# Layer norms with logarithm and exponential on ScalarE in place of a square root, a reciprocal and a spread, in a six-layer transformer stack

## The reference

```python
x = x + 0.5 * L0_ffn(layernorm(x))      # A: coupled feed-forward
x = x + L0_attn(layernorm(x))           # B: causal attention, and a layer norm of its own (M)
x = x + 0.5 * L0_ffn(layernorm(x))      # C
x = x + 0.5 * L1_ffn(layernorm(x))      # D: 8 experts, top 2, and a shared one
x = x + L1_attn(layernorm(x))           # E: full attention
x = x + 0.5 * L1_ffn(layernorm(x))      # F
def layernorm(x): return (x - mean(x)) / sqrt(var(x) + 1e-5)
```

## Time and profile before

| | |
|---|---|
| median of 3 runs | 1381.76 us (1378.12 to 1389.53) |
| the profiled execution's own time | 1379.58 us |
| its span, first to last instruction | 1377.9 us |
| granted TensorE clock, mean | 0.974 |
| busy: TensorE, VectorE, ScalarE, POOL | 96%, 84%, 77%, 12% of the span |
| loop of the first attention | about 94 to 469 us |
| loop of the second attention | about 653 to 1286 us |

### The profile page before, as it was taken

The page is one execution under the profiler, slowest core; times in us unless marked ns, Lnnn a source line. Parts: engine busy times, 40 slices in busy tenths (PEclk is TensorE's granted clock), DMA queues, the critical chain, the costliest instruction groups (busy, mean ns, idle before and its releaser), DMA issues.

```text
span 1377.9 us, 30123 instructions
## 1 busy us (share of the span) xinstructions
PE 1317.6 (96%) x11896; PEld 470.0 (34%) x11896; DVE 1164.0 (84%) x1537; ACT 1054.4 (77%) x2060; POOL 165.7 (12%) x441
## 2 busy tenths in 40 slices
PE   8889999999999997999899999999999999999989
PEld 4243333332333352535233333332333323333533
DVE  6768889999999267555899999999999999995454
ACT  4548888998999636334499999999999999998431
POOL 9225221111111000001100000000000000000000
PEclk9989999999999999999699999999999999999899
DMA  5242310200000012001311000000000000000000
GB/s 144 54 132 43 46 21 21 42 5 12 4 4 5 12 31 62 1 0 47 115 48 49 4 4 12 4 4 3 12 4 4 4 4 11 4 4 3 11 7 24
DMA packets 38524, 35.09 MB, mean 25 GB/s; under 512 B 16080, under 2 KB 31920, under 8 KB 38384
## 3 DMA queue, kind: packets, MB, share of 16 engines
q1 hardware_dynamic: 38384, 33.17, 10.0%
HBM read 17.03 MB, written 9.70 MB: 19 GB/s over the span
## 4 chain that ended last, share of the span: by engine, by line
PE 53%; DVE 41%; ACT 2%; issue 2%; SPq 1%; DMA 0%; POOL 0%; DVEq 0%; ACTq 0%
DVE m_blockmax L1418 36%; PE ps L1296 10%; PE ps L1241 9%; PE ps L1277 7%; PE ps L1300 6%; PE ps L614 3%; PE ps L625 3%; PE ps L615 2%; PE ps L248 2%; PE ps L241 1%; PE ps L331 1%; PE ps L1260 1%; PE ps L235 1%; DVE m_xn L510 1%; DVE m_prob L506 1%
## 5 line engine op out<-in xcount | busy, mean ns | idle before, releaser
L1418 DVE TENSOR_REDUCE m_blockmax<-ps 128x2 f32<-128x1024 f32 (+1 forms) x768 | 880.9, 1207 | 24.4 <-PE ps L1241 18.3
L1391 ACT ACTIVATE m_prob<-ps 128x512 f32<-128x512 f32 (+3 forms) x1664 | 845.8, 576 | 48.5 <-PE ps L1277 34.2
L1277 PE MATMUL ps<-m_q_max,m_k_all 64*128 64x512 bf16 (+3 forms) x1664 | 338.2, 368 | 0.5
L1241 PE MATMUL ps<-m_k_all,m_q_all 64*128 64x512 bf16 (+3 forms) x1664 | 319.2, 382 | 19.4 <-DVE m_blockmax L1418 16.1
L1300 PE MATMUL ps<-m_prob,m_v_op 128*16 128x256 f32 x4096 | 320.9, 385 | 0.1
L1241 PEld LDWEIGHTS ps<-m_k_all,m_q_all 64*128 64x128 bf16 x1664 | 79.7, 93 | 344.7 <-DVE m_blockmax L1418 173.1
L1296 PE MATMUL ps<-m_prob,m_v_op 128*16 128x256 f32 (+3 forms) x2560 | 179.6, 353 | 0.8 <-POOL m_prob L1461 0.3
L1277 PEld LDWEIGHTS ps<-m_q_max,m_k_all 64*128 64x128 bf16 x1664 | 143.0, 94 | 90.8 <-ACT m_prob L1391 47.7
L1300 PEld LDWEIGHTS ps<-m_prob,m_v_op 128*16 128x16 f32 x4096 | 67.1, 94 | 133.7 <-issue 101.3
L1442 POOL CAST m_maxparts<-m_negmax 128x8 bf16<-128x8 f32 x64 | 14.1, 220 | 725.8 <-DVE m_negmax L1426 721.2
L724 ACT ACTIVATE m_prob<-ps 128x512 f32<-128x512 f32 x40 | 23.5, 594 | 71.4 <-PE ps L614 71.3
(11 more groups left out here) (221 smaller groups left out, 1033.2 us busy)
## 6 DMA issues: line engine op xcount, KB each, us to landing
m_part<-m_xn SPq DMA_DIRECT2D x48, 128.0 KB, 2.3
ba_parts<-m_part SPq DMA_DIRECT2D x8, 384.0 KB, 3.4
ea_parts<-m_part SPq DMA_DIRECT2D x8, 384.0 KB, 2.6
m_k_all<-ea_parts SPq DMA_DIRECT2D x84, 32.0 KB
m_q_all<-ea_parts SPq DMA_DIRECT2D x84, 32.0 KB
m_k_all<-ba_parts SPq DMA_DIRECT2D x36, 64.0 KB
m_q_all<-ba_parts SPq DMA_DIRECT2D x36, 64.0 KB
ba_sums<-m_pv SPq DMA_DIRECT2D x128, 9.0 KB
```

The source lines that it names most:

```text
L1241: mm = pe.matmul(ps[:, MX + 2 * (u % 2) + j, 0:width], q_all[head, pair, q0:q0 + TW], k_all[head, pair, CW * kc:CW * kc + width], start=Tr ...
L1277: pe.matmul(ps[:, e % ST, q0:CW], k_all[head, pair, TW * i:TW * i + TW], q_max[m % 2][head, q0:CW], start=True, stop=True).then_inc(self.s ...
L1391: nc.scalar.activation(prob[:, (2 * t + j) % NP, q0:CW], ps[:, e % ST, q0:CW], ACT.Exp, scale=SCALE)\
L1418: nc.vector.tensor_reduce(blockmax[:, m % plan.AHEAD, qt, :, kc], ps[:, MX + 2 * (u % 2):MX + 2 * (u % 2) + 2, 0:width], AX.X, ALU.max)\
```

## The change

1. The variance of a chunk comes from one product of all 512 columns with the same matrix of 1/128 as the mean, so it stands in all rows. `var_of`, `row_of`, `std`, `pe_spread` and `dve_invert` of the norm are gone. ScalarE takes Ln of the variance plus eps from PSUM into `sq`, then Exp with scale -0.5 in place. The norm's multiplication reads `sq`.
2. The warming calls ask for Ln where they asked for Sqrt. Square and root of successive chunks alternate in a different order. In `b_end` there are seven phases, and the first layer of the feed-forward for chunks 0 and 1 stands in the last (`ffn_c.pe(pe, True)`).
3. In attention B the builds of the first three pairs come before or right after the last queries and keys, in other banks (0, 1, 4, 5), the values' products are taken out of the opening and put behind the second to fifth `fill`, SP loads the first group after the parts of chunk 0, and middle copies of chunks 2 and 3 stand last on ScalarE.

```diff
     def pe_var(self, pe, i, c, bank):
         pe.wait_ge(self.squared, NC * i + c + 1)
-        for u in range(TPC):
-            mm = pe.matmul(self.ps[0:32, bank, 0:TW], self.k["var_of"][:, u, :], tile(self.k["sq"], TPC * c + u),
-                           start=(u == 0), stop=(u == TPC - 1))
-        mm.then_inc(self.var_ready, 1)
-
-    def pe_spread(self, pe, i, c, bank):
...
+        pe.matmul(self.ps[:, bank, :], self.k["mean_of"][:, :], chunk(self.k["sq"], c), start=True, stop=True)\
+            .then_inc(self.var_ready, 1)
...
-    def dve_invert(self, dve, i, c):
-        dve.wait_ge(self.std_ready, NC * i + c + 1)
-        self.nc.vector.reciprocal(self.std[:, c, :], self.std[:, c, :]).then_inc(self.inverted, 1)
...
+    def dve_norm(self, dve, i, c, dst):
+        dve.wait_ge(self.inverted, NC * i + c + 1)
+        self.nc.vector.tensor_tensor(chunk(dst, c), chunk(self.k["cen"], c), chunk(self.k["sq"], c), ALU.mult)\
             .then_inc(self.out, 1)
...
     def act_root(self, act, i, c, bank):
         act.wait_ge(self.var_ready, NC * i + c + 1)
-        self.nc.scalar.activation(self.std[:, c, :], self.ps[0:32, bank, 0:TW], ACT.Sqrt, bias=self.k["eps"][0:32, 0:1])\
-            .then_inc(self.std_ready, 1)
+        sq = chunk(self.k["sq"], c)
+        self.nc.scalar.activation(sq, self.ps[:, bank, :], ACT.Ln, bias=self.k["eps"][:, 0:1]).then_inc(self.logged, 1)
+        act.wait_ge(self.logged, NC * i + c + 1)
+        self.nc.scalar.activation(sq, sq, ACT.Exp, scale=-0.5).then_inc(self.inverted, 1)
...
+    def with_values(self, order):
+        out, fills = [], 0
+        for o in order:
+            out.append(o)
+            if o[0] == "fill":
+                fills += 1
+                if 2 <= fills < 2 + NC:
+                    out.append(("values", fills - 2, 0))
+        return out
...
         if self.causal and b == 0:
             pe.wait_ge(self.k["constants"].made, Constants.SELECT_MADE)
-            pe.wait_ge(self.rest_ready, 2 * NC)
-            pe.wait_ge(self.v_ready, NC)
+            pe.wait_ge(self.rest_ready, 2)
...
                 pe.wait_ge(self.k_built, pair + 1)
-                pe.wait_ge(self.q_built, pair + 1)
+                pe.wait_ge(self.q_built, 3)
...
@@ TensorE's program, ahead of attention B @@
                 att_b.pe_queries_keys(pe, 2)
-                att_b.pe_values(pe, 1)
+                att_b.pe_build(pe, 0)
+                att_b.pe_build(pe, 1)
                 pe.wait_ge(norm.out, NC * LN_B + 4)
                 att_b.pe_queries_keys(pe, 3)
-                att_b.pe_values(pe, 2)
-                att_b.pe_values(pe, 3)
-                for b in range(6):
+                for b in range(2, 6):
                     att_b.pe_build(pe, b)
...
@@ ScalarE's program, ffn_end and ahead of attention B @@
-                    warm(ACT.Sqrt)
-                    for c in range(3):
-                        norm.act_square(act, ln, c)
+                    warm(ACT.Ln)
+                    norm.act_square(act, ln, 0)
+                    norm.act_square(act, ln, 1)
                     norm.act_root(act, ln, 0, bank)
+                    norm.act_square(act, ln, 2)
+                    norm.act_root(act, ln, 1, bank + 1)
                     norm.act_square(act, ln, 3)
-                    for c in range(1, NC):
-                        norm.act_root(act, ln, c, bank + c)
+                    norm.act_root(act, ln, 2, bank + 2)
+                    norm.act_root(act, ln, 3, bank + 3)
                     warm(then)
...
-                att_b.act_values(act, 0)
-                for c in (2, 3):
-                    att_b.act_high(act, c)
-                    att_b.act_middle(act, c)
-                    att_b.act_values(act, c - 1)
-                att_b.act_values(act, 3)
-                for b in range(1, 6, 2):
-                    att_b.act_build(act, b)
+                att_b.act_high(act, 2)
+                att_b.act_build(act, 1)
+                att_b.act_high(act, 3)
+                att_b.act_build(act, 3)
+                att_b.act_build(act, 5)
+                att_b.act_middle(act, 2)
+                att_b.act_middle(act, 3)
                 att_b.act_loop(act)
```

More of the change, by code:

```diff
@@ L364, in pe @@
                 w1(s, 1)
-            if s == self.start and not begun:
-                for c in (2, 3):
-                    self.norm.pe_spread(pe, self.ln, c, c)
             if s > self.start:
@@ L666, in pe @@
                 down(i - 1)
-            if i == 1 and before is not None:
-                norm.pe_spread(pe, self.ln, NC - 1, self.BC)
             if i + 2 < len(steps):
@@ L825, in dve @@
         best(0, 1)
-        if before is not None:
-            self.norm.dve_invert(dve, self.ln, last)
-        else:
+        if before is None:
             logits(1)
@@ L831, in dve @@
         if before is not None:
-            self.norm.dve_norm(dve, self.ln, last, self.xn, self.BC)
+            self.norm.dve_norm(dve, self.ln, last, self.xn)
         shared(2)
@@ L1632, in _ @@
                     norm.pe_var(pe, LN_A, c, c)
-                pe.wait_ge(constants.made, Constants.ROWS_MADE)
-                for c in (0, 1):
-                    norm.pe_spread(pe, LN_A, c, c)
                 ffn_a.pe(pe, False)
```

192 lines of the change are left out of this document (72 added, 120 removed).

## The result

| | before | changed |
|---|---|---|
| median | 1383.83 us (1378.12 to 1389.53, 4 runs) | 1436.42 us (1430.97 to 1441.45, 4 runs) |
| ratio, 95% interval | | 1.0386 (1.0357 to 1.0416) |
| profiled execution, own time and span | 1379.58, 1377.9 us | 1437.54, 1435.8 us |
| granted TensorE clock, mean | 0.974 | 0.947 |

The change makes the kernel 3.9% slower, some 53 us by the medians and 58 us between the two profiled executions. The forecast was 1425 us, its range 1397 to 1446.

A forecast was written before the change was run, and what follows sets the result against it. The ending chain was TensorE 53%, VectorE 41%, ScalarE 2%. With two table loads per chunk, stage terms of 38.5 us plus 6 for clock took 1379.6 to 1424.1; with half of a 2.2 us offset, 1425; range 1397 to 1446.

The forecast's parts named there:

- The rival of one table: All chunk norms: Ln and Exp share one table, no load between them; sum -10.6 us, 1371 us; chance 0.13.
- first norm and ffn A: First layer norm into the feed-forward: ScalarE's four Ln-Exp pairs delay the first Gelu to 27.8 us; +7.3 us.
- norm before, and loop B: First attention: first score +0.2 us, then four value products moved into the loop cost 4.3; +4.5 us.
- after the first attention: Eight chunk norms in diagonal order: ScalarE's loads and waits for VectorE delay the first Gelu; +19.5 us, the largest term.
- norm before the first experts: The experts' Exp moves 4.0 us later, followed down to +0.9 at the sixth gate; +1.5 us.
- norms before the second attention: Chunks 2 and 3 are two whole pairs ahead of the second high copy, 651.4 instead of 646.74; +4.7 us.
- last experts: Norms before the last experts: norm 1 comes 0.9 us later, and the router with it; +1.0 us.
- clock, apart: All stages: TensorE's added idle time lowers its clock, doubling the cost of some products; +6 us, between 0 and 20.
- the step that took the transfer and the Tanh as the last things ahead of VectorE's update: First feed-forward: VectorE's update, held before by a transfer until 28.90, now waits for the Tanh and starts at 36.2.
- covered by the three windows built on the spot: First attention: SyncE's loads go out some 5 us later, but the fourth window, first to read them, comes near 108.
- The rival of the cold TensorE: Two loads, half clock across the first three norm stages and into feed-forwards: +20 for +6, 1439; chance 0.12 with builds.
- The builds don't come early: First attention: builds wait for the third build of queries, losing 7 us, 1432; chance 0.12 together with cold TensorE.

The follow-up runs named there:

- the joint set: Changed kernel, with the table set holding both Ln and Exp loaded by name before the norms, two warming calls removed: 1375.03 us, ratio 0.9933.
- The two queue runs: Changed kernel with SyncE's group 1 loads behind the first two sendings of sums: 1451.84 us; changed kernel with four sums buffers instead of two: 1435.53 us.
- the kernel with the joint set in this place alone: Changed kernel with the Ln-and-Exp set loaded by name only ahead of the eight chunk norms after the first attention: 1415.94 us, ratio 1.0230.
- the fillers: Changed kernel plus TensorE products whose results nobody reads: 96 of them, 1425.70 us, ratio 1.0306; 34 around the last experts only, 1434.18 us.
- the kernel with four buffers: Kernel with the joint set, plus four buffers for the attentions' sums in place of two: 1373.40 us, ratio 0.9902.
- The kernel with two buffers: The kernel with the joint set, its attention sums still in two buffers: 1375.03 us, ratio 0.9933.
- the kernels with one load a chunk: Kernel with the joint set, loaded again at each chunk norm: behind the wait for the variance 1419.51 us, ratio 1.0235; ahead of it 1407.97 us, 1.0209.

## Why the prediction was right, and where it was not

The direction, the mechanism and the range held: 66 loads, two at each chunk norm, forecast 1425 us, measured 1436. The rival of one table was the case to fear, and the runs show what separated it: the joint set exists, since the program runs with it by name without a load between Ln and Exp, but it isn't chosen when each function is asked for by itself. The rule of the Trainium skill, "ScalarE: Activation LUTs", section on table sets (Ln then Exp is one load), disagrees with the changed kernel's trace, 28 loads at L268, and agrees only with the kernel that names the set. The drain of 1.38 us that the same page adds to a load ("What ACT_TABLE_LOAD costs") is in neither trace. Behind the load, 495.37 + 1.28 is 496.65, and the Exp starts at 496.67; ahead of the loads ScalarE stands idle 0.5 and 0.4 us in all 28 and 22 cases together.

By the forecast's own terms, in the profiled executions, each as the growth of the shift at that landmark:

| term | forecast | measured |
|---|---|---|
| first norm and ffn A | +7.3 | +10.2 |
| norm before, and loop B | +4.5 | +6.8 |
| after the first attention | +19.5 | +23.4 |
| norm before the first experts | +1.5 | +1.5 |
| norms before the second attention | +4.7 | +4.6 |
| last experts | +1.0 | +7.3 |
| clock, apart | +6 | in the rows above, and +3.5 in ffn C |

These sum to 57.3, and 0.6 us in loop E brings them to 57.9, the difference of the spans. The norms before the second attention are read at the copy that the forecast used (646.74 us before); by the first score, as in the stage table, they grew 6.4 us, and loop E shrank by 1.1.

*First norm.* The first Gelu came at 27.93 (forecast 27.8) and the first Tanh at 36.75 (35.6), so ScalarE's part was followed nearly right. (The forecast's own terms add up to 28.1: 11.20 + 14.2 + 1.3 less 0.3, and 1.7.) What failed is the step that took the transfer and the Tanh as the last things ahead of VectorE's update. The coupling constants, through three small activations queued on ScalarE among the Gelus, released VectorE only at 36.08, and the update started at 38.30 where 36.2 was forecast. 1.2 of these 2.1 us are the Tanh's own lateness (it ended at 37.44); the other 0.9 are the constants', since the update's first part, which needs them, stood from 37.19 to 38.37 ahead of it. A further 0.8 us of the +10.2 arose later in the feed-forward:

```profile
36.08 0.15 DVE L520 TENSOR_SCALAR af_u<-af_gt 128x1 f32<-128x1 f32 x1 [7.97 <-ACT af_gt L461]
...
38.30 1.14 DVE L484 SCALAR_TENSOR_TENSOR m_prob<-m_prob,af_c,m_part 128x512 f32<-128x512 f32 x1
```

What waited on the moved instructions was followed through the Tanh alone, not through the constants. That explains 0.9 of the 2.9 us by which the term fell short. For the Tanh's part the clock is the likely cause, though no run isolates it: from first Gelu to first Tanh the changed kernel took 8.8 us at a granted clock of 0.75, and the kernel with the joint set 7.4 at 1.00, with the same instructions.

*Before the first attention.* The opening itself was right: first high copy +7.2 in its stage as forecast, first score -0.5 where +0.2 was said, four value products costed at 4.3. The step that failed is the sentence that SyncE's later loads are "covered by the three windows built on the spot". It asked who reads the loads and not what stands behind them in the queue. The sums did, and ScalarE waited 5.15 us. The two queue runs bound it: the wait can't be exchanged away, and with the sums buffered it costs nothing only if the loads are in time too.

*After the first attention.* First Gelu +23.4 for +19.5. The kernel with the joint set in this place alone puts 18.6 us on the loads; the other 4.8 stay without them. The order followed had TensorE's steps at their lengths at full clock; in this stretch the clock was 0.76 where the forecast took 2.4 GHz for the sum and put 6 us aside for all stages together. The kernel before had 0.96 there, so the row gave no warning but that idle time lowers it, which the forecast said and priced too low.

*Last experts.* The failed size is the clock's again: +1.0 for ScalarE's part, where +7.3 was measured, and the same loads and instructions took 5.2 us less at a higher clock without fillers and 8.2 less with them. The kernel before had already 0.80 of the clock in these norms, which the forecast never asked for; its two clock rows are of other stretches.

Clock, taken together: the forecast's +6 against 11 us that the fillers took back in measured medians, and they don't reach ffn A. By the medians the term was mis-sized by about half. The low end of the estimate, 5 us, would agree with it, and no run shows more than its upper bound of 20.

The rival of the cold TensorE, 1439, is nearer to 1436 than the forecast. The half clock did reach into ffn C, as it said, and into the last experts; of its +20 the fillers account for 11, and the rest of its number is met by the queue and by ffn A's constants, which it didn't have. So that it lands nearer is in part luck. "The builds don't come early" was wrong: alone they bring the first score 7.3 us forward.

## What to carry to other kernels

Count the table loads before anything else when a change alternates two functions on ScalarE, and ask for the set that holds both by name: here three such calls, with two warming calls taken out, turned +3.9% into -0.7%. Where a step is moved, follow its queue to the end, past the readers of its own data to whatever is issued behind it. A price for idle time on TensorE belongs to the products that follow as well, and should be read from a stretch that already has such gaps.

## What was not expected of the hardware

- ffn C, with the same instructions, took 37.7 us at a granted clock of 0.94 in one profile and 45.2 at 0.73 in two others; ffn A between 37.2 at 1.00 and 48.0 at 0.71. In the kernel with four buffers TensorE stood idle 4.44 us ahead of C's second layer, and the next 20 us were granted 0.50, all of it the lower level:

```profile
505.79 1.98 PE L324 MATMUL ps<-m_part,m_cn_w 128*64 128x512 f32 x4 [4.44 <-ACT m_part L411]
```

  The kernel with two buffers had such an idle time too and 38.0 us, so what decides isn't settled.
- A load by name costs the same 1283 ns as one that was placed without a name, and is done again even if that set is already there (42 loads in the kernels with one load a chunk, 16 with the set loaded once a stage).
- The first 25 added loads cost 1.53 us each in the norm columns, more than their length, and the next 24 cost 1.0.
- A gain in one stage can go with a lower clock in the next: the four buffers gave 8 us in loop B, and in the same execution ffn C took 7 more.
